# Softmax sums of six attention rows from pre-added quarters: GpSimd takes adds, VectorE's steps and the end of the program are dealt out anew

## The chip, the cores and the metric

The kernel runs on one core of a Trainium2 chip, as one program launched once. The metric is the device time of that launch in microseconds (us). The core's engines work from their own queues, each in program order, and wait for each other by semaphores: TensorE (PE in the profile; its weight loads are PEld), VectorE (DVE), ScalarE (ACT), GpSimd (POOL), SyncE (SP, which here only issues transfers). Transfers run on 16 DMA engines.

## The reference

Two transformer layers over eight sequences of 512 tokens, 128 wide, all in float32:

```python
x = L0_attn_x                                    # (8, 512, 128)
xn = _layernorm(x)
x = x + _L0_attn_ref(xn, ...) + _L0_ffn_ref(xn, ...)   # one head without softmax, then a norm; fp4-quantised ffn
xn = _layernorm(x)
x = x + _L1_attn_ref(xn, ...) + _L1_ffn_ref(xn, ...)
...
def _L1_attn_ref(x, Wq, bq, Wk, bk, Wv, bv, Wo, bo):    # 16 heads of 64, one shared key and value head
    q = (x @ Wq + bq).reshape(B, S, H, DK); k = x @ Wk + bk; v = x @ Wv + bv
    scores = jnp.einsum('bshd,btd->bhst', q, k) / np.sqrt(DK)
    w = jax.nn.softmax(scores, axis=-1)
    out = jnp.einsum('bhst,btd->bshd', w, v).reshape(B, S, H * DV)
    return out @ Wo + bo
def _L1_ffn_ref(...):                            # 8 experts, the top 2 of each token, hidden width 512
```

## The kernel before

The kernel is one long software pipeline. A **row** (index r, 0 to 7) is one sequence's layer-1 attention; it has 64 **steps** (index k): 16 heads by 4 quarters of 128 keys. Beside row r the layer-0 work of row r + 1 is strung out over the same steps, at places given by hand-written tables: `L0_AT` for TensorE and ScalarE, `L0_DVE` for VectorE (each entry k lets the generator `l0` run on to its next `yield` at step k). Row 7 also holds 92 steps of the expert feed-forward (23 tiles of tokens by 4, behind k = 15, 23 and 31). Every engine walks the same list `steps`, so the order of each queue is fixed when the program is built.

A step of attention is: `first` on TensorE (scores of a quarter, transposed, two matmuls, L1478 and L1479) into one of two PSUM banks; `Exp` on ScalarE into `wide`, a ring of six SBUF buffers 128x512 (L878). Two heads make a **pair**, eight steps, and their quarters alternate: even k is head b = 0, odd k is b = 1. Two steps behind each fourth step `values` takes four `wide` buffers at once: eight matmuls of weights with values (L1506, 32 columns of stationary data each, into four column groups) and then four matmuls with `ones`, 128x32, that add up the weights over the keys (L1517). A pair has two such blocks, so a row has 16. The last two pairs (`direct`) use eight ones matmuls a block (L1514) so that the sums come out spread over all partitions. In the profile each of these float32 matmuls shows as two records (x16 and x8 in a block).

When a pair is done, ScalarE copies the values bank (`raw`, L904) and one step later the sums bank (`sraw`, L909); SP sends the sums through DRAM, VectorE inverts them 16 wide (L1246, L1247), SP spreads them back (`inv`), and VectorE scales (`on`, L1260). For the direct pairs VectorE inverts the whole bank (L1264). `project` multiplies by Wo (L1538).

The row maximum for the exponent comes from a second set of scores (L1432) that VectorE reduces (`mneg`, L1066), two reductions at every other step, through a ring of four PSUM banks that also serves all of the layer-0 work; TensorE turns the maxima (L1437), ScalarE copies them and a transfer puts them beside the queries (`q_lm<-mrow`).

GpSimd computes inverse roots for the three norms of a row (`root`, L661: VectorE gives the variance at L952 and takes the root at L956), clears `x_rows` (L688), scatters routed tokens by indirect transfers (L702), and in row 0 subtracts the rounded half of 16 staged expert weights 128x512 (L726), whose inputs SP loads (`stage`) and whose results it stores (`w_rows`). At the start of row 7 SP loads the first four tiles' expert weights, 1 MB each (`WEIGHTS_AT`, `load_tile_weights`, L577), and GpSimd the first tiles' tokens `x_m`.

## Time and profile before

| | before |
|---|---|
| median of 3 runs | 1312.55 us (1308.25 to 1314.61) |
| profiled execution | 1308.08 us, span 1306.5 us |
| TensorE busy | 1220.1 us, 93% |
| VectorE busy | 955.3 us, 73% |
| ScalarE busy | 681.7 us, 52% |
| GpSimd busy | 264.3 us, 20% |
| TensorE clock, mean | 0.974 of full |

The span is the time from the first to the last instruction of the core; the profiled execution's own time is 1.58 us above it. Busy time counts an engine's instructions without its waits.

### The profile page before, as it was taken

The numbers are of one execution on the slowest core, as the hardware profiler recorded it, in microseconds if no ns is written. First come the engines' busy times: TensorE is split into PE (matmuls) and PEld (weight loads), VectorE is DVE, ScalarE is ACT, GpSimd is POOL, SyncE is SP. The second block draws the span as 40 slices with busy tenths as digits, with TensorE's granted clock in tenths as the row PEclk, the third lists the DMA queues.
The fourth block names the chain that finished last, engine by engine and source line by source line (L and its number), as shares of the span: only waits on it lengthen the run. The fifth ranks groups of instructions, "written<-read, shape, count | busy, mean of one in ns | idle before, by whom it ended". The sixth has DMA issues, their size and how long they took to land.

```text
span 1306.5 us, 21963 instructions
## 1 busy us (share of the span) xinstructions
PE 1220.1 (93%) x7185; PEld 722.9 (55%) x7185; DVE 955.3 (73%) x2332; ACT 681.7 (52%) x1252; POOL 264.3 (20%) x315
## 2 busy tenths in 40 slices
PE   5459989999999999999999999999999999999997
PEld 3235445555555555555554555555555458787743
DVE  6876787578857885788578857875687668677866
ACT  4136545644464456444644464456444468687731
POOL 2033222200220022002200220022000307273730
PEclk9669998999999999999999999999999989999999
DMA  3073666223422253225322432243222567476371
GB/s 81 1 194 97 205 195 194 75 72 78 139 67 67 68 147 75 67 67 139 83 67 67 140 83 67 66 140 83 67 67 67 146 202 241 153 248 198 120 218 59
DMA packets 99763, 150.59 MB, mean 115 GB/s; under 512 B 35340, under 2 KB 51276, under 8 KB 95684
## 3 DMA queue, kind: packets, MB, share of 16 engines
q1 hardware_dynamic: 84772, 115.53, 33.1%
q0 software_dynamic: 11664, 32.69, 7.8%
q10 hardware_dynamic: 3216, 0.97, 0.3%
q8 instruction: 59, 0.97, 0.3%
q14 instruction: 52, 0.43, 0.1%
HBM read 59.86 MB, written 38.68 MB: 75 GB/s over the span
## 4 chain that ended last, share of the span: by engine, by line
PE 66%; DVE 17%; DMA 4%; issue 4%; ACT 4%; POOL 2%; SPq 2%; ACTq 0%; DVEq 0%; POOLq 0%
PE bank L1506 14%; PE bank L1478 7%; PE bank L1517 6%; PE bank L1432 5%; PE bank L1479 5%; PE bank L1334 4%; PE bank L1336 4%; PE bank L1335 4%; DVE mneg L1066 4%; PE bank L1538 3%; PE bank L1350 2%; ACT wide L878 2%; PE bank L1340 2%; PE bank L1396 1%; PE bank L1375 1%
## 5 line engine op out<-in xcount | busy, mean ns | idle before, releaser
L878 ACT ACTIVATE wide<-bank 128x512 f32<-128x512 f32 x512 | 294.8, 599 | 319.5 <-PE bank L1479 319.2
L1066 DVE TENSOR_REDUCE mneg<-bank 128x1 f32<-128x512 f32 x512 | 328.8, 684 | 146.5 <-PE bank L1432 142.3
L1478 PE MATMUL bank<-q_hh,k_hl 128*128 128x512 f32 x512 | 233.5, 456 | 17.8 <-ACT wide L878 14.1
L1506 PE MATMUL bank<-wide,v_w 128*32 128x512 f32 x2048 | 248.1, 602 | 1.0 <-issue 1.0
L1479 PE MATMUL bank<-q_lm,k_h 65*128 65x512 f32 x512 | 203.8, 398 | 0.0
L1478 PEld LDWEIGHTS bank<-q_hh,k_hl 128*128 128x128 f32 x512 | 96.8, 189 | 139.8 <-issue 78.3
L661 POOL TENSOR_TENSOR rs<-rs,power 128x4 f32<-128x4 f32 x24 | 24.5, 1020 | 616.6 <-DVE rs L952 616.5
L1517 PE MATMUL bank<-wide,ones 128*32 128x512 f32 x992 | 129.1, 592 | 0.0
L740 POOL DMA_INDIRECT y_rows<-y_m,to_u x92 | 103.3, 1123 | 105.0 <-DVE y_m L1192 83.0
L1506 PEld LDWEIGHTS bank<-wide,v_w 128*32 128x32 f32 x2048 | 53.8, 109 | 123.0 <-issue 115.2
L1432 PE MATMUL bank<-k_a,q_x 128*128 128x512 f32 x256 | 106.5, 416 | 4.7 <-ACT hqt L798 2.7
L1432 PE MATMUL bank<-k_b,q_x 128*128 128x512 f32 x256 | 102.6, 401 | 4.2 <-DVE mneg L1066 4.2
L1479 PEld LDWEIGHTS bank<-q_lm,k_h 65*128 65x128 f32 x512 | 97.6, 191 | 11.3 <-issue 1.4
L702 POOL DMA_INDIRECT x_rows<-xr,slot_u x64 | 63.0, 984 | 164.1 <-DVE slot_u L1138 129.7
L904 ACT ACTIVATE raw<-bank 128x512 f32<-128x512 f32 x64 | 38.3, 598 | 100.2 <-PE bank L1517 91.0
L1300 DVE TENSOR_TENSOR part_l<-wide,part_h 128x512 fp32r<-128x512 f32 x92 | 61.9, 689 | 32.6 <-ACT wide L883 32.2
L883 ACT ACTIVATE part_h<-bank,b_t 128x512 fp32r<-128x512 f32 x92 | 63.4, 689 | 22.9 <-PE bank L1336 16.1
L1517 PEld LDWEIGHTS bank<-wide,ones 128*32 128x32 f32 x992 | 32.3, 110 | 74.6 <-issue 74.6
L1538 PE MATMUL bank<-wo,on 128*128 128x128 f32 x512 | 61.4, 279 | 4.8 <-DVE on L1260 4.8
L1538 PEld LDWEIGHTS bank<-wo,on 128*128 128x128 f32 x512 | 60.9, 195 | 7.4 <-DVE on L1260 6.2
L1432 PEld LDWEIGHTS bank<-k_a,q_x 128*128 128x128 f32 x256 | 49.0, 191 | 25.9 <-ACT q_x L808 12.8
L883 ACT ACTIVATE wide<-bank,b_t 128x512 f32<-128x512 f32 x92 | 63.0, 685 | 0.0
(253 smaller groups left out, 1938.4 us busy)
## 6 DMA issues: line engine op xcount, KB each, us to landing
q_hh<-q_x SPq DMA_DIRECT2D x256, 128.0 KB
w_t<-w_rows SPq DMA_DIRECT2D x23, 1024.0 KB, 4.7
x_rows<-part_h POOLq DMA_DIRECT2D x65, 258.0 KB, 5.0
q_lm<-q_rest SPq DMA_DIRECT2D x128, 128.0 KB
inv<-inverse_scratch SPq DMA_DIRECT2D x124, 128.0 KB, 2.9
w_rows<-w_t SPq DMA_DIRECT2D x8, 1024.0 KB, 5.0
x_m<-x_rows SPq DMA_DIRECT2D x19, 258.0 KB, 3.8
stage<-in_L_ffn_W SPq DMA_DIRECT2D x16, 256.0 KB, 4.9
```

Of the source, the lines that this page charges most:

```text
L702: pool.indirect_dma_start(x_rows, bass.IndirectOffsetOnAxis(ap=slot_u[:, b, i:i + 1], axis=0), xr[:, i, :], None).then_inc(scattered, 16)
L740: pool.indirect_dma_start(y_rows, bass.IndirectOffsetOnAxis(ap=to_u[:, t % TO, i:i + 1], axis=0), y_m[:, t % YM, i, :], None).then_inc(y_s ...
L878: act.activation(wide[:, st.g % WIDE, :], ps, ACT.Exp, scale=SCALE1).then_inc(wide_full, 1)
L883: ins = act.activation(dst, ps, ACT.Gelu_apprx_tanh, bias=b_t[:, st.t % WT, st.m:st.m + 1])
L1066: dve.tensor_reduce(mneg[:, pair % 2, col:col + 1], ps[:], X, ALU.max, negate=True).then_inc(free, 1)
L1300: dve.tensor_tensor(part_l[:, y % PARTS, :], wide[:, st.g % WIDE, :], part_h[:, y % PARTS, :].bitcast(F32), ALU.subtract).then_inc(lo_done, 1)
L1432: into(("mx", 2 * pair + b, j), lambda ps: pe.matmul(ps[:], q_x[:, pair % 2, P * j:P * j + P], keys[:, n % 2, :], start=True, stop=True))
L1478: pe.matmul(ps, k_hl[:, n, t], q_hh[:, gh % HEADS, :], start=True, stop=False)
L1479: last = pe.matmul(ps, k_h1[0:DK + 1, n, t], q_lm[0:DK + 1, gh % HEADS, :], start=False, stop=True)
L1506: pe.matmul(ps_out[0][rows, :], v_w[:, n, c, TILE * d:TILE * d + TILE], weights, start=(c == 0), stop=(c == TT - 1))
L1517: last = pe.matmul(ps_out[1][rows, :], ones[:], weights, start=(half == 0), stop=(half == 1))
L1538: last = pe.matmul(ps[:, P * i:P * i + P], on[:, g % (H // 4), P * i:P * i + P], wo[:, g, :], start=(g == pairs.start), stop=(g == pairs.s ...
```

## The change

In rows 1 to 6 (pairs 8 to 55, `added`) GpSimd adds, at each step with k % 4 of 2 or 3, the `wide` buffer of two steps earlier to the present one, as two instructions of 128x256 (`halve`), into `halves`. One step after the last values block of the pair TensorE does four ones matmuls on these sums (`sums_of`) in place of the eight that its two blocks had. ScalarE's `Exp` waits for the add before it overwrites a `wide` buffer, and its copy `sraw` moves one step back. GpSimd's program is dealt out over the steps: roots, scatters and clears stand at given steps among the adds. `halves` and `stage` lie over `x_m`, and the expert weights of row 0 turn over four buffers rather than two.

VectorE's table `L0_DVE` is new: the norm of layer-0 attention with its scale and shift runs at k = 5 to 8 rather than 29 to 37, the quantisation of `xn` starts at k = -4 rather than -7, and the variance of two norms is given out earlier. The turning of the maxima moves from the sixth to the fifth step of a pair. In row 7 the direct pairs do ones ahead of values, the last projection is split after pair 6 rather than 5, and three of the four first expert weights are loaded at k = -2, -1 and 1. Row 7 keeps its ones matmuls on `wide`.

```diff
-    LAST_NORM_AT = {6: ATT, 7: ATT + 3}
-    LAST_WO_AT = [None, ATT, ATT + 4]
+    LAST_NORM_AT = {6: ATT, 7: ATT + 2}
+    LAST_WO_AT = [None, ATT + 2, ATT + 3]
...
-    WEIGHTS_AT = [2, 5, 10, 12]
+    ROWS_AT, WEIGHTS_AT = 2, [-2, -1, 1, 13]
...
+    FIRST_HALVED, LAST_HALVED = H // 2, (NB - 1) * (H // 2)
+    ROOT_AT = [6, 42, 51]
+    SCATTER_AT = [[1, 4, 5, 8], [13, 16, 17, 20]]
+    ZERO_AT = [24, 25, 28, 29, 32, 33, 36, 37]
...
+    def added(pair):
+
+        return FIRST_HALVED <= pair < LAST_HALVED
...
+    def adds(st):
+
+        return st.kind == "o" and st.k % TT >= 2 and added(pair_of(st))
...
-        if s == TT + 1 and 0 <= here + 1 < total:
-            events.append(("mt", here + 1))
...
+        if s == TT and 0 <= here + 1 < total:
+            events.append(("mt", here + 1))
...
+            def halve(st):
+
+                half, b, pair = st.k % PAIR // TT, st.k % 2, pair_of(st)
+                if pair > FIRST_HALVED:
+                    pool.wait_ge(summed, pair - FIRST_HALVED)
+                pool.wait_ge(wide_full, st.g + 1)
+                for q in range(2):
+                    cols = slice(S // 2 * q, S // 2 * q + S // 2)
+                    last = pool.tensor_tensor(halves[:, half, b, cols], wide[:, (st.g - 2) % WIDE, cols],
+                                              wide[:, st.g % WIDE, cols], ALU.add)
+                last.then_inc(halved, 1)
...
                     if st.g >= WIDE:
                         act.wait_ge(second_done, st.g - WIDE + 1)
+                        if st.g - WIDE in add_of:
+                            act.wait_ge(halved, add_of[st.g - WIDE])
...
+            def sums_of(pair):
+
+                free_bank(("ps", pair))
+                pe.wait_ge(halved, add_of[last_step(2 * pair + 1)])
+                for half in range(2):
+                    for b in range(2):
+                        rows = slice(DK * b + TILE * half, DK * b + TILE * half + TILE)
+                        last = pe.matmul(ps_out[1][rows, :], ones[:], halves[:, half, b, :], start=True, stop=True)
+                last.then_inc(summed, 1)
...
-                pairs = (slice(0, 4), slice(4, 8 if r < NB - 1 else 6), slice(6, 8))[part]
+                pairs = (slice(0, 4), slice(4, 8 if r < NB - 1 else 7), slice(7, 8))[part]
...
+                pair = pair_end(st, 1)
+                if pair is not None and added(pair):
+                    sums_of(pair)
```

TensorE's queue at a pair's end in row 1, before: values (L1506) and ones (L1517) stand together after every fourth step.

```order
L1506 MATMUL bank<-wide,v_w 32x512 x8
L1517 MATMUL bank<-wide,ones 32x512 x4
L1478 MATMUL bank<-q_hh,k_hl 128x512
L1479 MATMUL bank<-q_lm,k_h 128x512
L1432 MATMUL bank<-k_a,q_x 128x512
L1432 MATMUL bank<-k_b,q_x 128x512
L1334 MATMUL bank<-x_h,wq_h 128x512
```

The same place in the changed kernel (L1589 is values, L1559 the ones matmuls of `sums_of`, L1536 and L1537 the scores):

```order
L1589 MATMUL bank<-wide,v_w 32x512 x8
L1536 MATMUL bank<-q_hh,k_hl 128x512
L1537 MATMUL bank<-q_lm,k_h 128x512
L1490 MATMUL bank<-k_a,q_x 128x512
L1490 MATMUL bank<-k_b,q_x 128x512
L1392 MATMUL bank<-x_h,wq_h 128x512
L1393 MATMUL bank<-x_l,wq_h 128x512
L1394 MATMUL bank<-x_h,wq_l 128x512
L1619 MATMUL bank<-wo,on 128x128 x16
L1559 MATMUL bank<-halves,ones 32x512 x4
```

The ones matmuls have left both blocks of the pair and stand once, a step behind the second.

VectorE's queue at the end of a row, before (L923 to L938 are the quantisation of `xn`, L1124 and L1126 the routing slots):

```order
L1118 TENSOR_TENSOR gsel<-gsel,gs 128x32
L923 TENSOR_REDUCE qs<-xn 128x32
L924 TENSOR_SCALAR qs<-qs 128x32
L925 RECIPROCAL qs<-qs 128x32
L927 TENSOR_SCALAR qs<-qs 128x32
L1124 TENSOR_TENSOR ahead<-ahead,bank 128x8 x4
L1126 TENSOR_TENSOR slot<-ahead,bank 128x32
L930 TENSOR_TENSOR t_66<-xn,qs 128x512
L932 TENSOR_SCALAR t_67<-t_66 128x512
L1066 TENSOR_REDUCE mneg<-bank 128x1 x2
L1059 SCALAR_TENSOR_TENSOR q_rest<-bank,bq_two,q_x 128x512
```

and in the changed kernel, where L1124 is now the reduction of maxima, L1182 and L1184 the slots, L982 to L991 the quantisation:

```order
L1176 TENSOR_TENSOR gsel<-gsel,gs 128x32
L1124 TENSOR_REDUCE mneg<-bank 128x1 x2
L1182 TENSOR_TENSOR ahead<-ahead,bank 128x8 x4
L1184 TENSOR_TENSOR slot<-ahead,bank 128x32
L1117 SCALAR_TENSOR_TENSOR q_rest<-bank,bq_two,q_x 128x512
L982 TENSOR_REDUCE qs<-xn 128x32
L983 TENSOR_SCALAR qs<-qs 128x32
L984 RECIPROCAL qs<-qs 128x32
L986 TENSOR_SCALAR qs<-qs 128x32
L989 TENSOR_TENSOR t_66<-xn,qs 128x512
L991 TENSOR_SCALAR t_67<-t_66 128x512
```

Six instructions of the quantisation have moved behind a pair of maxima and the rest of a query.

TensorE's queue at the very end, before (L1514 ones of a direct pair, L1538 projection):

```order
L1478 MATMUL bank<-q_hh,k_hl 128x512
L1479 MATMUL bank<-q_lm,k_h 128x512
L1538 MATMUL bank<-wo,on 128x128 x8
L1506 MATMUL bank<-wide,v_w 32x512 x8
L1514 MATMUL bank<-wide,ones 32x512 x8
L1538 MATMUL bank<-wo,on 128x128 x8
```

and now:

```order
L1536 MATMUL bank<-q_hh,k_hl 128x512
L1537 MATMUL bank<-q_lm,k_h 128x512
L1582 MATMUL bank<-wide,ones 32x512 x8
L1589 MATMUL bank<-wide,v_w 32x512 x8
L1619 MATMUL bank<-wo,on 128x128 x16
```

The ones come first, and all 16 matmuls of the second projection (12 for pairs 4 to 6, 4 for pair 7) stand behind the values.

## Rows read from the trace of the kernel before

**Rows 1.** Stretches: start:end, length, busy us of each engine, clock, DMA share

```profile
501.00:633.00 132.00, 130.01 (x803) 73.50 (x802) 97.76 (x249) 68.27 (x129) 15.61 (x22) 1.00 0.36 88
...
603.00:623.00 20.00, 19.91 (x134) 12.86 (x133) 17.08 (x57) 8.68 (x17) 5.57 (x10) 1.00 0.62 148
623.00:633.00 10.00, 10.00 (x53) 5.21 (x53) 7.30 (x22) 7.64 (x12) 3.28 (x4) 1.00 0.53 146
```

**Rows 2.** The chain that ended last, two rows' worth: start, us, what

```profile
490.83 1.98 PE bank L1350 x4
...
622.75 1.98 PE bank L1350 x4
```

**Rows 3.** The same chain from 600 to 732 us

```profile
600.43 0.86 PE bank L1517 x8
...
717.22 0.86 PE bank L1517 x8
...
718.98 0.30 DVE xres L1007
...
722.73 1.02 POOL rs L661
```

**Rows 4.** Groups of instructions: busy us, mean ns, idle before

```profile
L1517 PE MATMUL bank<-wide,ones 128*32 128x512 f32 x992 | 129.1, 592 | 0.0
...
L726 POOL TENSOR_TENSOR w_t<-stage,w_t 128x512 fp32r<-128x512 f32 x16 | 20.6, 1288 | 68.5 <-ACT w_t L847 68.5
```

**Rows 5.** Timeline of GpSimd in row 0: start, us, instruction

```profile
162.35 2.56 POOL L726 TENSOR_TENSOR w_t<-stage,w_t 128x512 fp32r<-128x512 f32 x2
```

**Rows 6.** Timeline of VectorE in the same stretch

```profile
127.22 1.49 DVE L937 TENSOR_TENSOR t<-t,t 128x352 f32<-128x352 f32 x1
128.74 0.52 DVE L938 TENSOR_TENSOR t<-t,t 128x352 f32<-128x352 f32 x1
...
162.39 1.23 DVE L956 SCALAR_TENSOR_TENSOR rs<-rs 128x4 f32<-128x4 f32 x1
163.66 1.27 DVE L957 TENSOR_TENSOR rs<-rs 128x4 f32<-128x4 f32 x1
164.96 0.16 DVE L958 SCALAR_TENSOR_TENSOR rs<-rs 128x4 f32<-128x4 f32 x1
...
188.40 1.20 DVE L952 TENSOR_SCALAR rs<-mv 128x4 f32<-128x4 f32 x1
```

**Rows 7.** Timeline of VectorE at the end of a row

```profile
618.39 0.69 DVE L923 TENSOR_REDUCE qs<-xn 128x32 f32<-128x512 f32 x1
...
621.54 0.43 DVE L932 TENSOR_SCALAR t<-t 128x512 uint32<-128x512 uint32 x1
```

**Rows 8.** Timelines of SP, VectorE and TensorE at the start of row 7

```profile
1035.38 0.38 SPq L577 DMA_DIRECT2D w_t<-w_rows  x1
...
1038.13 0.59 SPq L533 DMA_DIRECT2D sums_scratch<-sraw  x1
...
1046.74 0.17 DVE L1246 TENSOR_TENSOR sums<-sums 128x16 f32<-128x16 f32 x1 [8.28 <-DMA sums<-sums_scratch]
...
1047.80 0.79 PE L1432 MATMUL bank<-k_b,q_x 128*128 128x512 f32 x1 [4.15 <-DVE mneg L1066]
...
1050.57 3.24 PE L1506 MATMUL bank<-wide,v_w 128*32 128x512 f32 x16
```

**Rows 9.** Waits from 105 to 237 us: total us, times, longest

```profile
ACT w_t L847 <- DMA stage<-in_L_ffn_W: 18.0, 7, 6.6
```

**Rows 10.** Timeline of all engines at the end of the program

```profile
1289.73 2.05 PE L1538 MATMUL bank<-wo,on 128*128 128x128 f32 x16 [0.62 <-DVE on L1260]
1291.71 1.92 PE L1506 MATMUL bank<-wide,v_w 128*32 128x512 f32 x16
...
1293.45 1.90 PE L1514 MATMUL bank<-wide,ones 128*32 128x512 f32 x16
...
1295.44 3.36 DVE L1264 RECIPROCAL inv_d<-bank 128x512 f32<-128x512 f32 x1 [2.94 <-PE bank L1514]
...
1299.58 3.40 PE L1538 MATMUL bank<-wo,on 128*128 128x128 f32 x16 [4.23 <-DVE on L1260]
1303.03 0.69 DVE L1235 TENSOR_TENSOR xres<-xres,bank 128x512 f32<-128x512 f32 x1 [3.50 <-PE bank L1538]
```

More of the change, by code:

```diff
@@ L281, in two_layers @@
     ring = Ring(SMALL, small_order)
+    add_of, count = {}, 0
+    for st in steps:
+        if adds(st):
+            count += 1
+            add_of[st.g] = add_of[st.g - 2] = count
     out_place, out_uses = {}, [0] * OUTB
@@ L573, in load_tile_weights @@
                     sp.wait_ge(table_set, 1)
+                    for i in range(WT):
+                        sp.wait_ge(w_stored[i], E // WT * 16)
                 ew = sp.value_load(tb_u[0:1, 1, t:t + 1], min_val=0, max_val=E - 1)
@@ L708, in load_first_rows @@
                 pool.wait_ge(scattered, 2 * TT * NB * 16)
+                pool.wait_ge(summed, LAST_HALVED - FIRST_HALVED)
                 for t in range(XT):
@@ new lines, in _ @@
+            for n in range(2):
+                for e in range(E):
+                    zero(n, e)
+            root()
+            for st in steps:
+                if st.kind == "o":
+                    if st.k in (ROOT_AT if st.r < NB - 2 else ROOT_AT[0:2] if st.r == NB - 2 else ()):
+                        root()
+                    if adds(st):
+                        halve(st)
+                    if st.r == 0 and st.k in SPLIT_STEPS:
+                        split_rest(SPLIT_STEPS.index(st.k))
+                    for b, at_ in enumerate(SCATTER_AT if st.r < NB - 1 else LAST_SCATTER_AT):
+                        for i in range(TT):
+                            if st.k == at_[i]:
+                                scatter(st.r, b, i)
+                    if st.k in ZERO_AT and st.r + 2 < NB:
+                        zero(st.r + 2, ZERO_AT.index(st.k))
+                    if st.r == NB - 1 and st.k == ROWS_AT:
+                        load_first_rows()
+                if st.g is not None:
+                    here, i = divmod(st.g - 3, TT)
+                    if here - 2 in tile_of:
+                        scatter_y(tile_of[here - 2], i)
@@ L905, in _ @@
                 pair = pair_end(st, 1)
-                if pair is not None and not direct(pair):
+                if pair is not None and not direct(pair) and not added(pair):
                     act.wait_ge(second_done, last_step(2 * pair + 1) + 1)
+                    act.wait_ge(sums_stored[pair % 2], 16 * (pair // 2))
+                    act.activation(sraw[:, pair % 2, :], ps_out[1][:], ACT.Identity).then_inc(out_free[1], 1)
+                pair = pair_end(st, 2)
+                if pair is not None and added(pair):
+                    act.wait_ge(summed, pair + 1 - FIRST_HALVED)
                     act.wait_ge(sums_stored[pair % 2], 16 * (pair // 2))
@@ L1493, in values @@
                 if half == 0:
-                    for name in (("pv", pair), ("ps", pair)):
-                        b, uses = out_place[name]
-                        if uses:
-                            pe.wait_ge(out_free[b], uses)
+                    free_bank(("pv", pair))
+                    if not added(pair):
+                        free_bank(("ps", pair))
                     if st.k == TT - 1:
@@ L1500, in values, with weights @@
                 pe.wait_ge(wide_full, st.g + 1)
+                def weights(c, b):
+                    return wide[:, (st.g - 3 + 2 * (c % 2) + b) % WIDE, :]
+                if direct(pair):
+                    for c in range(2 * half, 2 * half + 2):
+                        for b in range(2):
+                            for d in range(2):
+                                rows = slice(DK * b + TILE * d, DK * b + TILE * d + TILE)
+                                last = pe.matmul(ps_out[1][rows, :], ones[:], weights(c, b), start=(c == 0), stop=(c == TT - 1))
+                    if half:
+                        last.then_inc(summed_up, 1)
@@ L1508, in values @@
+                        if added(pair) or direct(pair):
+                            last.then_inc(second_done, 1)
+                if added(pair) or direct(pair):
+                    return
                 for c in range(2 * half, 2 * half + 2):
                     for b in range(2):
-                        weights = wide[:, (st.g - 3 + 2 * (c % 2) + b) % WIDE, :]
-                        if direct(pair):
-                            for d in range(2):
-                                rows = slice(DK * b + TILE * d, DK * b + TILE * d + TILE)
-                                last = pe.matmul(ps_out[1][rows, :], ones[:], weights, start=(c == 0), stop=(c == TT - 1))
-                        else:
-                            rows = slice(DK * b + TILE * (c % 2), DK * b + TILE * (c % 2) + TILE)
-                            last = pe.matmul(ps_out[1][rows, :], ones[:], weights, start=(half == 0), stop=(half == 1))
@@ L1518, in values @@
-                        last.then_inc(second_done, 1)
+                        rows = slice(DK * b + TILE * (c % 2), DK * b + TILE * (c % 2) + TILE)
+                        pe.matmul(ps_out[1][rows, :], ones[:], weights(c, b), start=(half == 0), stop=(half == 1))\
+                            .then_inc(second_done, 1)
             def second(st):
@@ L1592, in _ @@
                     values(block_end(st))
+                pair = pair_end(st, 1)
+                if pair is not None and added(pair):
+                    sums_of(pair)
                 past = behind(st, LAG)
```

122 lines of the change are left out of this document (58 added, 64 removed).

## The prediction

> **What bounds the kernel now.** I read the busy times of whole rows first, then the chain that ended last, then the timelines of the places it passes. A row of attention repeats every 131.9 us (622.75 less 490.83, the same piece of the chain in two rows [rows 2]). In such a row TensorE is busy 130.0 of 132 us and VectorE 97.8 [rows 1]: TensorE bounds, with 2.0 us of idle time. The chain says the same for most of a row: 13 of its 16 blocks of ones matmuls lie on it, from 600.43 to 717.22, at 0.86 us each [rows 3]. But in two stretches it goes over VectorE: the end of the row, where VectorE is busy 17.1 of 20 us [rows 1], and some ten more from 718.98 on, with one hop over GpSimd's root of 1.02 us [rows 3]. TensorE is nearly full there too, so both engines are at the limit together. A faster TensorE meets VectorE in those 30 of 132 us first.
>
> **The change, part by part.**
>
> *Ones matmuls, rows 1 to 6.* A pair had two blocks of 0.86 us and gets one. That is 0.86 us of TensorE's work a pair, 6.9 a row, 41.3 in six rows. As a cross-check, all 124 such blocks take 129.1 us busy [rows 4], 1.04 each with the overlap at their ends. Only the 13 blocks on the chain count at once: 13 x 0.43 = 5.6 us a row. The other three lie under VectorE.
>
> *GpSimd's adds.* Each row has 32 adding steps of two instructions of 128x256. The nearest row is its subtraction 128x512 at 1.288 us [rows 4]; half of that is 0.64 us, so 64 x 0.64 = 41 us a row. The upper bound is that a short one costs what the root on 128x4 costs, 1.02 us [rows 3], 65 us a row. I take 0.64: the subtraction shows a cost that goes with its columns, and the root is another operation. With its present 15.6 us [rows 1] GpSimd is busy 57 to 81 of some 126 us. An Exp overwrites the buffer four steps after the add may start, 4 x 2.06 = 8.2 us, against 1.3 to 2.0 for a step's two adds and 1 or 2 us of a scatter or a root in front of them. I charge 0.5 us a row for late adds.
>
> *What the adds do to VectorE.* The trace shows two engines in each other's way. While two subtractions run on GpSimd from 162.35 for 2.56 us [rows 5], two VectorE instructions on 128x4, with inputs from SBUF, take 1.23 and 1.27 us where their successor takes 0.16, and at 127.22 one takes 1.49 where its twin takes 0.52 [rows 6]. The wait shows inside the duration. From 127.22 to 188.40 I find 8 such instructions, 6.2 us too long in total, beside 15 subtractions: 0.41 us for each. An add of half the length is met half as often and for half as long (0.10 us), or just as often for half as long (0.21 us): 6.6 to 13.1 us a row in 64 adds. VectorE's load rises from 97.8 to between 104 and 111 us. In the 30 of 132 us on the path that is 1.5 to 3.0 us; I take 2.1. The Trainium skill, "SBUF — State Buffer", section "Who interferes with whom", says that a VectorE instruction with two SBUF inputs, or in a two-port mode, and a GpSimd instruction that reads SBUF shut each other out for a whole instruction, whichever starts first; the stretched rows agree. By its letter the wait is at most one add, 0.64 us, which is the end of my range and not beyond it. The same skill, "GPSIMD Engine Reference", section 4.1, advises against elementwise work on GpSimd as about twice as slow; here its slowness matters only if the queue is late.
>
> *VectorE dealt out anew.* The six instructions of the quantisation that leave the end of the row take 3.58 us from first to last with the slots between them [rows 7], of which 2.5 are theirs. The variance of two norms goes out earlier, so two hops over GpSimd of about 1.1 us (one is the 1.02 us [rows 3]) fall away. That would be 4.7 us of VectorE's stretches. TensorE lies close underneath: its 2.0 us idle and the three hidden blocks' 1.3 us are all that can be won, 3.3. With 2.1 us of waits for GpSimd against 4.7, the net is -2.6. The 2.5 us go to the next ten microseconds, where VectorE is busy 7.3 [rows 1]; with 0.7 us of new waits it has 10.5 us of work in 9.1, so 1.3 us come back. Net -1.3 a row. The norm of attention moves from k = 29 to 37, where the chain is TensorE's, to k = 5 to 8, where it is too: nothing by itself, room for the new waits. In the remaining 100 us of a row some 7.5 us of new waits lie in VectorE's idle time; if that cover were gone they would cost all of it. I charge 1.0.
>
> Sum of a row: -5.6 - 1.3 + 0.5 + 1.0 = -5.4 us, six rows **-32.4 us**. The later `sraw` leaves five steps, ten microseconds, to the sums' way through DRAM: nothing. The turning of maxima one step earlier waits for a reduction that the ring of banks asks for at the same step anyway: nothing.
>
> *End of the program.* Before, projection (2.05), values (1.92), ones (1.90), then VectorE's inversion of 3.36 us while TensorE stands idle 4.23 us and comes back slow, 3.40 us for a projection whose twin took 2.05, then an addition of 0.69 [rows 10]. Now the block starts at about 1289.8 without the projection in front: ones to 1291.6, inversion to 1295.0, scaling to 1295.7; meanwhile values to 1293.5 and twelve matmuls of projection (2.7 us, by the 16 records' 1.8 for eight) to 1296.2, then four (0.9) to 1297.1, addition to 1297.8. The old addition ends at 1303.7: **-5.9 us**. The first direct pair's inversion can start 0.6 us earlier, before VectorE's own work holds it: **-0.6**.
>
> *Start of row 7.* SP issues a 1 MB weight load at 1035.38, directly in front of the sums' store at 1038.13; VectorE gets them at 1046.74 after 8.28 us of waiting, TensorE stands 4.15 us and then runs a values block in 3.24 us instead of 1.92 [rows 8]. The loss is 4.15 + 1.3 and about 1.3 more on neighbours, some 6.8 us. The three loads now start at k = -2, some 12 us ahead of the store. GpSimd's loads of `x_m` stay. I take **-5.0**, between 0 (the three loads queue up in front of it all the same) and -6.8.
>
> *Row 0.* 2 MB of clears move into the steps where expert weights are staged, for which ScalarE waits 18.0 us already [rows 9]. Bounds 0 and 5 us; **+1.5**, as the four buffers may take a wait away.
>
> Total: -32.4 - 5.9 - 0.6 - 5.0 + 1.5 = -42.4 us. The span of 1306.5 becomes 1264.1, the execution's 1308.08 becomes 1265.7. The median of the runs before is 4.5 us above its profiled execution, the fastest run equal to it; I keep **1266 us**.
>
> **The rivals.**
>
> *All of TensorE's saving is real* (0.14). VectorE's idle time takes every wait: -6.9 x 6 - 6.5 - 6.8 = -54.6, 1253 us. For it speaks that VectorE idles 34 of 132 us; against it that in 603 to 623 it idles only 3 [rows 1].
>
> *VectorE becomes the bound in longer stretches* (0.22). Half of the upper 13.1 us, 6.6, lies on the path instead of 3.1: +3.5 a row, +21, 1287 us. For it speaks the load of 111 in 126 us, 88%, and a ring of four banks that lets TensorE run ahead by only one pair of maxima.
>
> *VectorE bound throughout: slower* (0.07). Place: VectorE against the adds; price: all 13.1 us a row on the path, and some 4 us of its own maxima held up behind them, 17.1 instead of 3.1: +84 - 42, 1350 us. It decides when the waits on the path pass 3.1 + 42.4/6 = 10.2 us a row. Against it speaks that the maxima's reductions (one PSUM input) are nowhere stretched in row 0.
>
> *GpSimd's queue holds the Exp* (0.05): a root or scatter waits in order for VectorE, and adds behind it. It costs what exceeds the 8.2 us; at 3 us for each of three roots a row, 54 us, 1320 us, slower by 0.6%. Less of it, 1 us each, gives 1284.
>
> **How the numbers follow.** The forecast (0.52) has its own range 1258 to 1277. The range for all is 1252 to 1290: it takes in the first two rivals and leaves out under 2 in 10. Within 0.5% (6.6 us), about what a measurement of this kernel can tell from no change, lie only parts of the last two: 0.03. Slower: the third rival and some of the last, 0.09. Faster: 0.88.
>
> **What would show it.** Right: a row period near 126.5 us, 192 fewer ones matmuls, adds of about 0.64 us, TensorE idle 3 to 4 us a row, single VectorE instructions of 0.16 us stretched to 0.5 to 0.8, the last inversion ending 3.8 us earlier with TensorE busy beside it, no idle time of 4 us near the start of row 7. Wrong: Exp waiting for `halves`; reductions of maxima as long chains in the middle of rows; adds of 1 us; a period above 129.

## The result, and the profile after

The changed kernel takes 1317.86 us (median of 6 runs, 1316.16 to 1320.66), the kernel before, run beside it, 1312.42 us (6 runs, 1308.25 to 1314.61). The ratio is 1.005, 95% interval 1.0036 to 1.0063: half a per cent slower, where 1266 us was forecast. The profiled execution has a span of 1314.3 us, 7.8 more than before.

The page: busy us, share of the span, instructions; then the chain's shares and the group of the adds (busy us, mean ns | idle before).

```profile
PE 1207.7 (92%) x6801; PEld 704.0 (54%) x6801; DVE 1012.3 (77%) x2332; ACT 683.2 (52%) x1252; POOL 551.0 (42%) x699
...
PE 70%; DVE 19%; issue 4%; DMA 3%; ACT 2%; POOL 2%; SPq 1%; ACTq 0%; DVEq 0%; POOLq 0%
...
L744 POOL TENSOR_TENSOR halves<-wide 128x256 f32<-128x256 f32 x384 | 290.2, 780 | 369.7 <-PE bank L1559 217.8
```

TensorE lost 12 us of work, VectorE has 57 us more with no instruction of its own added, GpSimd 287 more. The stretches that answer to [rows 1], and two in the middle of the next row:

```profile
501.00:633.00 132.00, 126.76 (x744) 70.83 (x742) 108.63 (x252) 70.08 (x133) 64.63 (x86) 1.00 0.33 89
603.00:623.00 20.00, 19.37 (x125) 12.52 (x124) 17.32 (x50) 10.25 (x20) 8.57 (x12) 1.00 0.24 55
623.00:633.00 10.00, 10.00 (x54) 4.86 (x51) 9.41 (x26) 6.42 (x11) 4.08 (x6) 1.00 0.18 58
662.00:670.00 8.00, 6.95 (x39) 2.97 (x32) 7.69 (x18) 3.53 (x7) 3.31 (x5) 1.00 0.08 24
670.00:680.00 10.00, 7.24 (x39) 3.23 (x41) 9.83 (x16) 3.39 (x8) 8.34 (x10) 0.95 0.50 136
```

VectorE goes from 97.8 to 108.6 us in 132. The end of the row is now no tighter than the middle: from 662 to 680 VectorE has half a microsecond free, TensorE stands, and the mean granted clock of the last stretch is 0.95. Taken by itself, the piece behind the stall runs at half the clock, which is the lower of its two levels, 1.2 GHz:

```profile
678.90:682.30 3.40, 3.40 (x18) 0.60 (x16) 3.19 (x9) 1.03 (x3) 0.96 (x1) 0.50 0.14 44
```

In the chain, the same piece of projection in two following rows:

```profile
499.29 2.64 PE bank L1408 x6
...
629.68 2.65 PE bank L1408 x6
...
761.68 2.67 PE bank L1408 x6
```

It returns after 130.4 and 132.0 us, against 131.9 in [rows 2]; the chain's row jitters by a place, so below I use score matmuls: their first step in rows 1 and 6 starts at 248.1 and 907.0, against 239.3 and 899.0 before. A row takes **131.8 us; it took 131.9**. Six rows gave nothing.

Where the 7.8 us arose, from the start of the first score matmul of steps (after less before, us; the parts are rounded). Here and below such a stretch is read from one profiled execution of each kernel, which lies up to 4.5 us from the median of its runs:

| stretch | forecast | measured |
|---|---|---|
| row 0 | +1.5 | +8.8 |
| rows 1 to 6 | -32.4 | +0.3 |
| row 7, k = 0 to 16 | -5.0 | +3.2 |
| row 7, k = 16 to 56 | 0 | +2.1 |
| from there to the end | -6.5 | -6.5 |

Inside a row the gain is there and is lost again: from k = 24 to 48 a row wins 3.4 us, from k = 56 to 64 0.9, and from k = 16 to 24 it loses 4.2. The timeline of all engines there (start, us, instruction, idle before); it answers to nothing in [rows 3], since before this place was TensorE's alone:

```profile
659.71 2.80 POOL L744 TENSOR_TENSOR halves<-wide 128x256 f32<-128x256 f32 x4 [2.56 <-ACT wide L932]
659.77 0.69 DVE L1015 SCALAR_TENSOR_TENSOR rs<-rs 128x4 f32<-128x4 f32 x1
660.50 0.66 DVE L1016 TENSOR_TENSOR rs<-rs 128x4 f32<-128x4 f32 x1
661.18 0.66 DVE L1017 SCALAR_TENSOR_TENSOR rs<-rs 128x4 f32<-128x4 f32 x1
...
673.71 3.79 POOL L744 TENSOR_TENSOR halves<-wide 128x256 f32<-128x256 f32 x4 [0.83 <-ACT wide L932]
673.74 1.09 DVE L997 TENSOR_TENSOR t<-t,t 128x352 f32<-128x352 f32 x1
674.86 0.93 DVE L1000 TENSOR_TENSOR sg<-t,qs 128x352 f32<-128x352 f32 x1
675.72 1.21 DVE L1318 TENSOR_TENSOR on<-raw,inv 128x512 f32<-128x512 f32 x1
676.85 1.27 DVE L1124 TENSOR_REDUCE mneg<-bank 128x1 f32<-128x512 f32 x2
677.58 0.86 PE L1460 MATMUL bank<-wu,xqt 128*128 128x352 f32 x2 [2.76 <-DVE mneg L1124]
...
679.34 3.39 PE L1589 MATMUL bank<-wide,v_w 128*32 128x512 f32 x16
```

While four adds run (0.70 us each), each 128x4 instruction of VectorE lasts almost as long as an add, where it took 0.16 us before; the larger ones behind them are stretched too. The maxima of the next pair (L1124) come behind them; TensorE stands 2.76 us for these, and its next block of values takes 3.39 us instead of 1.92.

### The profile page after: what moved, and what is told of

It is laid out like the page before. It is cut to its first block, busy times and chain, and to the rows that moved or that the text cites. A ratio compares the mean times of both kernels' runs of the same rounds, so it can differ in the third digit from the quotient of the medians.

```text
span 1314.3 us, 21803 instructions
## 1 busy us (share of the span) xinstructions
PE 1207.7 (92%) x6801; PEld 704.0 (54%) x6801; DVE 1012.3 (77%) x2332; ACT 683.2 (52%) x1252; POOL 551.0 (42%) x699
## 4 chain that ended last, share of the span: by engine, by line
PE 70%; DVE 19%; issue 4%; DMA 3%; ACT 2%; POOL 2%; SPq 1%; ACTq 0%; DVEq 0%; POOLq 0%
PE bank L1589 15%; PE bank L1536 8%; PE bank L1537 6%; PE bank L1490 6%; DVE mneg L1124 5%; PE bank L1392 5%; PE bank L1619 4%; PE bank L1394 4%; PE bank L1393 4%; PE bank L1559 3%; PE bank L1408 2%; PE bank L1398 2%; PE bank L1443 2%; PE bank L1454 2%; PE bank L1433 1%
## 5 line engine op out<-in xcount | busy, mean ns | idle before, releaser
L932 ACT ACTIVATE wide<-bank 128x512 f32<-128x512 f32 x512 | 298.2, 598 | 337.7 <-PE bank L1537 305.1
L744 POOL TENSOR_TENSOR halves<-wide 128x256 f32<-128x256 f32 x384 | 290.2, 780 | 369.7 <-PE bank L1559 217.8
L1124 DVE TENSOR_REDUCE mneg<-bank 128x1 f32<-128x512 f32 x512 | 328.3, 682 | 128.8 <-PE bank L1490 125.0
L1589 PE MATMUL bank<-wide,v_w 128*32 128x512 f32 x2048 | 257.4, 622 | 0.0
L1536 PE MATMUL bank<-q_hh,k_hl 128*128 128x512 f32 x512 | 239.3, 467 | 15.4 <-ACT wide L932 12.6
L1537 PE MATMUL bank<-q_lm,k_h 65*128 65x512 f32 x512 | 205.2, 401 | 0.0
L1536 PEld LDWEIGHTS bank<-q_hh,k_hl 128*128 128x128 f32 x512 | 97.3, 190 | 155.0 <-issue 82.4
L752 POOL DMA_INDIRECT y_rows<-y_m,to_u x92 | 98.0, 1066 | 103.1 <-DVE y_m L1250 81.7
L1589 PEld LDWEIGHTS bank<-wide,v_w 128*32 128x32 f32 x2048 | 55.5, 112 | 132.0 <-issue 124.9
L1537 PEld LDWEIGHTS bank<-q_lm,k_h 65*128 65x128 f32 x512 | 98.5, 192 | 9.4 <-issue 1.4
L860 ACT ACTIVATE q_x<-bank,bq_two 128x512 fp32r<-128x512 f32 x64 | 44.0, 687 | 45.9 <-PE bank L1394 45.4
L1490 PEld LDWEIGHTS bank<-k_b,q_x 128*128 128x128 f32 x256 | 49.1, 192 | 24.0 <-DVE mneg L1124 12.8
```

The lines of the kernel that those rows point to most:

```text
L744: last = pool.tensor_tensor(halves[:, half, b, cols], wide[:, (st.g - 2) % WIDE, cols], wide[:, st.g % WIDE, cols], ALU.add)
L752: pool.indirect_dma_start(y_rows, bass.IndirectOffsetOnAxis(ap=to_u[:, t % TO, i:i + 1], axis=0), y_m[:, t % YM, i, :], None).then_inc(y_s ...
L932: act.activation(wide[:, st.g % WIDE, :], ps, ACT.Exp, scale=SCALE1).then_inc(wide_full, 1)
L1124: dve.tensor_reduce(mneg[:, pair % 2, col:col + 1], ps[:], X, ALU.max, negate=True).then_inc(free, 1)
L1490: into(("mx", 2 * pair + b, j), lambda ps: pe.matmul(ps[:], q_x[:, pair % 2, P * j:P * j + P], keys[:, n % 2, :], start=True, stop=True))
L1536: pe.matmul(ps, k_hl[:, n, t], q_hh[:, gh % HEADS, :], start=True, stop=False)
```

## The experiments

**Adds almost taken away; the deal taken back; the deal alone.** The first leaves GpSimd's adds and waits in place and cuts each to 4 columns, so most of the sums are left out; in the first added pair it fills the rest of `halves` with ones:

```diff
+                if pair == FIRST_HALVED:
+                    for q in range(2):
+                        pool.memset(halves[:, half, b, S // 2 * q + 4:S // 2 * q + S // 2], 1.0)
...
-                    cols = slice(S // 2 * q, S // 2 * q + S // 2)
+                    cols = slice(S // 2 * q, S // 2 * q + 4)
```

> The changed kernel with each of GpSimd's adds cut from 256 columns to 4, all waits and semaphores kept (the sums of weights of rows 1 to 6 are then wrong: nearly all of halves keeps the value 1). It takes away the time that the adds hold VectorE and leaves the new deal of VectorE's work. Theory A, the waits for GpSimd's adds eat the saving: VectorE busy falls from 108 to about 98 us a row, the stalls of TensorE at steps 10 to 12 and 16 to 18 vanish, the row's period falls from 132.0 to about 126, the whole to about 1283 us. Theory B, the new deal packs too much of VectorE's work into steps 5 to 17 and would stall without any add: the period stays at 130 or above, the whole above 1305 us.

The second has VectorE's work at its old steps, in the changed kernel; the third has it at the new steps, in the kernel before, with one root in row 0 moved ahead to match:

```diff
-    L0_DVE = [-14, -13, -11, -10, -4, -4, -3, -2, 0, 0, 5, 6, 7, 8, 8, 10, 11, 13, ...
-    ROOT_AT = [6, 42, 51]
+    L0_DVE = [-14, -11, -11, -10, -7, -6, -4, -2, 0, 0, 9, 10, 13, 17, 18, 21, 25, ...
+    ROOT_AT = [30, 43, 53]
...
-                if n:
-                    yield from attended(18)
-                    yield 18
-                    scale_and_shift()
...
```

> The changed kernel with the old table of VectorE's steps, the norm of attention back at steps 29 to 37 and GpSimd's roots at steps 30, 43 and 53 to match; the adds stay whole. Theory A: waits for the adds stay and fall elsewhere, period 130 to 132, the whole about 1315 us. Theory B: steps 5 to 17 have room again, no stall at step 16, period about 127 to 128, the whole about 1290 us.

> The kernel before with the new deal of VectorE's work alone (GpSimd's second root in row 0 moved to before its first subtraction, so that nothing waits in a circle). Theory A: without adds the deal does no harm, period 131 to 132, the whole 1308 to 1313 us. Theory B: the stall at step 16 is there without adds, period 134 to 136, the whole 1325 us or more.

Measured: 1285.93 us without most of the adding (ratio to the kernel before 0.979, 0.977 to 0.981); 1357.71 with the old deal (1.033, 1.031 to 1.035); 1312.24 for the new deal alone (1.000, 0.998 to 1.001). The adds therefore cost 32 us. Rows 1 to 6 take 758.8 us without real adds, 784.0 before and 784.3 in the changed kernel: 25.5 of the 32 us lie there, all that these rows had saved, and 5.6 more in steps 0 to 16 of row 7 (81.4 us against 87.1). The deal is worth nothing by itself and 40 us beside the adds: theory B, that it causes a stall without any add, fell. The result with the old deal was in neither theory's range. The deal does decide where the adds' waits stop TensorE: with the old one steps 16 to 24 take 16.2 us (16.8 before the change), but steps 32 to 40 take 18.8 (15.9) and steps 56 to 64 27.1 (20.9; means of rows 1 to 5). With the old deal a row takes 140.0 us ((935.38 - 375.47) / 4 in the chain, the same piece of projection), and that piece itself runs slow:

```profile
375.47 5.23 PE bank L1409 x6
...
935.38 5.17 PE bank L1409 x6
```

**The size of an add.** The three kernels differ from the changed one only in the pieces of a step's add; the sums are the same.

```diff
-                for q in range(2):
-                    cols = slice(S // 2 * q, S // 2 * q + S // 2)
+                for q in range(4):
+                    cols = slice(S // 4 * q, S // 4 * q + S // 4)
```

> The changed kernel with each add as four instructions of 128x128 rather than two of 128x256. The total of columns is the same. If VectorE waits for the rest of one GpSimd instruction: the single wait halves (at most some 0.43 instead of 0.73 us), but GpSimd's fixed cost of 0.15 us a piece makes it busy 9 to 10 us a row more; VectorE busy a row falls from 107 to about 104 us, the whole 5 to 15 us faster. If VectorE waits for the whole stream of adds (GpSimd takes the pair back at once): VectorE's busy time stays or rises and the whole is 1318 us or slower.

> The changed kernel with each add as one instruction of 128x512. If VectorE waits for the rest of one GpSimd instruction: single waits of up to 1.28 us, VectorE busy a row rises from 107 to 109 to 112 us, the whole 5 to 20 us slower. If it waits for the whole stream: no change within 4 us.

> The changed kernel, each step's adds in eight instructions of 128x64 instead of two of 128x256. The same sums. So far 512 columns gave 1335, 256 gave 1318, 128 gave 1293 us, and adds of 4 columns (two a step) 1286. Theory (VectorE's small instructions wait for the rest of one GpSimd instruction, so its length sets the price): an add should take about 0.30 us (0.45 for 128 and 0.73 for 256 columns give 0.16 us fixed and 0.0022 a column), eight 2.4 us a step, GpSimd busy about 95 us a row, and each wait is at most 0.3 us: 1283 to 1293 us. Rival 1 (what counts is the share of time in which GpSimd works, since each new instruction can slip in ahead of VectorE): more waits, not shorter ones in sum, 1293 to 1320. Rival 2: GpSimd's queue gets late, as 2.4 us a step with a root or a scatter is more than a step of 2.06 us: over 1300, and ScalarE or the ones matmuls wait for the sums.

One row of each in its trace, from 633 us on, with the adds of 512, 256, 128, 64 and 4 columns in this order (start:end, length, busy us of TensorE, weight load, VectorE, ScalarE, GpSimd, clock, DMA):

```profile
633.00:767.16 134.16, 126.08 (x729) 69.81 (x733) 108.95 (x247) 68.27 (x129) 58.43 (x53) 0.99 0.32 87
```

```profile
633.00:764.79 131.79, 126.58 (x738) 70.07 (x737) 107.05 (x249) 68.28 (x130) 64.14 (x85) 0.99 0.33 89
```

```profile
633.00:761.41 128.41, 125.13 (x738) 69.89 (x738) 104.78 (x249) 68.52 (x130) 74.81 (x150) 1.00 0.34 91
```

```profile
633.00:762.04 129.04, 125.14 (x738) 69.62 (x737) 108.05 (x249) 68.44 (x129) 96.82 (x278) 1.00 0.35 90
```

```profile
633.00:761.15 128.15, 124.63 (x738) 70.37 (x737) 97.57 (x248) 68.86 (x130) 28.96 (x86) 1.00 0.34 91
```

| columns of an add | time, us | ratio to before | row, us | VectorE's waits a row |
|---|---|---|---|---|
| 512 | 1335.36 | 1.019 (1.016 to 1.022) | 134.2 | 11.4 |
| 256 | 1317.86 | 1.005 (1.004 to 1.006) | 131.8 | 9.5 |
| 128 | 1292.90 | 0.985 (0.984 to 0.987) | 128.4 | 7.2 |
| 64 | 1295.32 | 0.987 (0.984 to 0.991) | 129.0 | 10.5 |
| 4 (sums left out) | 1285.93 | 0.979 (0.977 to 0.981) | 128.2 | 0 |

The last column is VectorE's busy time less the 97.57 us of the row without real adds. One reads two things. The waits are 7 to 11 us whatever the length; what they cost the row is 6.0, 3.6, 0.3 and 0.9 us. And TensorE's own busy time in the same 738 matmuls is 124.63 without adds and 126.58 with those of 256: of the 3.6 us, 2.0 are matmuls that run longer, and the 3.4 us at half the clock account for 1.7 of them. The quarters gained 25 us, more than the 5 to 15 expected; whole adds lost 17, as expected. Below 128 columns nothing more is won, and the two times do not differ clear of their intervals: an add of 64 still takes 0.316 us (0.453 for 128), GpSimd works 97 of 129 us, and VectorE's waits rise from 7.2 to 10.5 us. So the theory of the length was right in direction, and its 1283 to 1293 for 64 columns was a little too low; the measured time lies in the range of rival 1, the share of time. The 7 us between 128 and 4 columns lie mostly at the start of row 7, whose steps 0 to 16 take 88.4, 87.1, 86.1, 85.9 and 81.4 us in the order of the table. There an add's length matters little.

**Row 0's clears.** They go from steps 24 to 37, among the staging of expert weights, to 54 to 61:

```diff
+                    zero_at = ZERO_AT if st.r else [54, 55, 56, 57, 58, 59, 60, 61]
```

> The changed kernel with GpSimd's eight clears of row 0 moved from steps 24 to 37 to steps 54 to 61, behind the staging of expert weights. If the clears delay the staged weights (ScalarE waited 7.12 us for one at 160.9): the 7.2 us that row 0 loses between steps 32 and 34 vanish and the whole is about 1311 us. If the staging waits for something else (the stores of 1 MB, the turning over four buffers): no change, 1318 us.

1315.51 us (1.002, 0.9998 to 1.003). Row 1 begins 2.9 us late instead of 8.8, so the clears are 6 of the 8.8 in this pair of traces. In all traces, row 1 begins at 247.0 to 250.6 us in the nine kernels with the new adds and the early clears, and at 242.0 to 244.9 in the five with late ones. By the medians the whole kernel got 2.4 us of it, less than the 7 of the first theory. In the changed kernel's row 0 ScalarE waits for a staged weight, an Exp stands behind it in its queue, and TensorE waits for that:

```profile
168.00 0.63 ACT L899 ACTIVATE w_t<-stage 128x512 fp32r<-128x512 f32 x1 [7.12 <-DMA stage<-in_L_ffn_W]
...
169.16 0.80 PE L1536 MATMUL bank<-q_hh,k_hl 128*128 128x512 f32 x1 [7.03 <-ACT wide L932]
```

**The maxima turned one step later, as before.**

```diff
-        if s == TT and 0 <= here + 1 < total:
+        if s == TT + 1 and 0 <= here + 1 < total:
```

> The changed kernel with the turning of maxima back at the sixth step of a pair. At the end of row 7 TensorE waits 3.05 us for a reduction before it (step 52), as VectorE still adds expert outputs. If that wait is new with the earlier place: the 2.9 us between steps 52 and 53 of row 7 vanish, rows 1 to 6 move by under 0.5 us each, the whole about 1315 us. If VectorE is the bound wherever the turning stands: the 2.9 us stay and the whole is 1318 us.

1322.29 us (1.007, 1.005 to 1.010). The wait that it was to remove is this one, in row 7 of the changed kernel, and it went:

```profile
1279.55 0.29 PE L1495 MATMUL bank<-ident,mneg 128*8 128x128 f32 x1 [3.05 <-DVE mneg L1124]
1280.63 3.12 PE L1582 MATMUL bank<-wide,ones 128*32 128x512 f32 x16
```

But another came in its place, five steps earlier, for the transfer of the turned maxima, with slow matmuls behind it:

```profile
1278.99 0.77 PE L1536 MATMUL bank<-q_hh,k_hl 128*128 128x512 f32 x1 [2.26 <-DMA q_lm<-mrow]
```

Steps 44 to 56 of row 7 take 26.0 us with the late turning and 26.2 with the early one, and the whole of row 7 281.9 and 282.0: in the last row the place of the turning is worth nothing. Rows 1 to 5 got 1.7 us longer each (133.5), row 6 1.5 shorter. Neither number of the expectation (1315, 1318) came out, and the ratio's interval overlaps that of the changed kernel.

**The start of row 7 as before.**

```diff
-    TABLE_CUTS = [59, 59, 60, 61]
-    ROWS_AT, WEIGHTS_AT = 2, [-2, -1, 1, 13]
+    TABLE_CUTS = [58, 59, 59, 62]
+    ROWS_AT, WEIGHTS_AT = 2, [2, 5, 10, 12]
```

> The changed kernel with the tiles' table computed at steps 58, 59, 59 and 62 and the first expert weights loaded at steps 2, 5, 10 and 12 of row 7, as before. If the table's chain on VectorE and the three early loads of 1 MB cost the start of row 7: the 9.7 us that it loses up to step 10 shrink to the 5 us that the kernel before lost at step 12, the whole 3 to 6 us faster, about 1313 us. If the late start is only VectorE's general delay by the adds: no change, 1318 us.

1317.77 us (1.003, 1.001 to 1.005): as the changed kernel. Steps 0 to 16 of row 7 took 86.4 us, against 87.1 changed and 83.9 before. Without real adds they took 81.4: it is the adds again that ate a gain of 2.5 us, by which way is open.

**No adds where the stall is.** Pairs 1 and 2 of rows 1 to 6 keep their 16 ones matmuls:

```diff
-        return FIRST_HALVED <= pair < LAST_HALVED
+        return FIRST_HALVED <= pair < LAST_HALVED and pair % (H // 2) not in (1, 2)
```

> The changed kernel without adds for the second and third pair of each row 1 to 6 (steps k = 8 to 23), whose sums go over 16 ones matmuls in TensorE again, as before the change; the adds of the other six pairs as they are (128x256). The same sums. TensorE gets 2 x 0.86 = 1.7 us a row of work back. Theory (the price is paid at one place, where VectorE is busy without a gap from k = 16 to 24 with the norm of attention and the quantisation, and TensorE loses 4 to 5 us there and part of its clock): the stall goes, a row costs 132 + 1.7 - 4.5 = 129, 6 rows 17 us less, 1300 us. Rival (VectorE is behind over the whole row, and the stall moves to the next tight place): the row keeps 132 or gets 1.7 us longer, 1318 to 1328 us.

1304.23 us (0.992, 0.989 to 0.996), a row 130.0 us. Steps 16 to 24 take 16.8 us again, as before the change (21.0 changed); steps 8 to 16 take 15.9, where both kernels took 13.5 to 14.0. So about half of the stall moved to the steps ahead, and neither theory's number came out (1300, or 1318 and more). Its five runs spread from 1297.9 to 1308.6 us, and the profiled one is the slowest. The place was rightly named, though: the row won 1.8 us with a quarter of the adds gone, and that beside giving up a quarter of the saving of 3.8, or 1.7 us if one counts the two blocks at 0.86. By this estimate these adds carried 2.8 to 3.5 us of a price of 3.6.

**The improvements together.**

> The changed kernel with three edits that seemed good one by one: adds in four instructions of 128x128 (1293 alone), the eight clears of row 0 at steps 54 to 61 (row 1 then began 6 us earlier, end 2 us earlier), and the turning of the maxima one step later, in the last row alone, as before the change (the wait of 3 us before the transposition vanished when it was done for all rows, but each row lost 1.3). The output is the reference's. If the three are independent: 1293 - 5 - 2.5 = 1285 us. If row 1 waits for VectorE whatever precedes it, the clears give only 2 us and the sum is 1289. If none adds up, 1293. Slower than before (over 1313) would say that the clears disturb the shorter adds.

1290.52 us (0.984, 0.980 to 0.987), 2.4 less than the quarters alone: the edits do not add up to the 7 us hoped for. In the traces row 1 begins 3.5 us earlier than with the quarters alone, which is the clears; row 7 takes 281.0 us against 281.2, so the late turning there gave next to nothing. In the profile of this kernel the start of row 7 still takes 86.6 us, and the last four scatters and the loads of tile rows are late. Three more kernels build on it. The first leaves the last pair of row 6 out of the adding, the second issues the tiles' weights later, the third does both:

```diff
-    FIRST_HALVED, LAST_HALVED = H // 2, (NB - 1) * (H // 2)
+    FIRST_HALVED, LAST_HALVED = H // 2, (NB - 1) * (H // 2) - 1
...
-    ROWS_AT, WEIGHTS_AT = 2, [-2, -1, 1, 13]
+    ROWS_AT, WEIGHTS_AT = 2, [2, 5, 10, 12]
```

> The kernel with quarters of 128x128, row 0's clears at steps 54 to 61 and the late turning in the last row (1290.5 us), and in it the last pair of row 6 without adds: its sums go over 16 ones matmuls again. The output is the reference's. In the profiles, the last four scatters of tokens stand in GpSimd's queue behind that pair's last adds (first scatter 2.7 us after the slots are there, against 1.0 before the change) and the rows of the first tile are loaded 25.6 us after row 7 began, against 14.6 before. Theory Q (GpSimd's order is what makes row 7 begin its tiles late): 0.9 us more of ones matmuls, scatters 2 to 3 us earlier, net 1 to 2 us less: 1288.5 to 1289.5. Rival D (the landing of scatters among 3 MB of weights sets it, or the first tile is not on the path at all): 1290.5 to 1291.5.

> The kernel with quarters of 128x128, row 0's clears at steps 54 to 61 and the late turning in the last row (1290.5 us), and in it the weight loads of the first three tiles issued at steps 2, 5 and 10 of row 7, as before the change, instead of -2, -1 and 1. The output is the reference's. In the profile of the changed kernel SP waits for the table of tiles with the loads (1040.49 to 1047.67) while the next pair's queries are ready at 1044.1; their DMAs are issued at 1047.78, and TensorE waits 2.5 us for them. Theory S (the waits of SP for the table hold the queries behind them): that wait of TensorE vanishes, the begin of the second pair of row 7 comes 2 to 3 us earlier; if the sums' way does not become late in its place, 1287.5 to 1288.5. Rival (the loads come later and meet the sums' store and load again, as in the kernel before, where VectorE waited 8.28 us for them): 1290.5 or up to 3 us more.

> The two edits before it together, over the same three: the last pair of row 6 without adds, and the weight loads at steps 2, 5 and 10 of row 7. The output is the reference's. If both theories hold: 1290.5 - 1.5 - 2.5 = 1286.5 us. If neither, 1291. If the second alone, 1289.

The kernel before took 1316.84 us beside these (1311.9 to 1319.01). One edit: 1293.83 us (0.983, 0.981 to 0.986); the other: 1295.30 (0.985, 0.982 to 0.987); both: **1289.81 us (0.980, 0.978 to 0.982)**, the best of the kernels that compute all sums. The expectations had 1287.5 to 1293.5 for the single edits and 1286.5 to 1291 for both. Alone, neither moved the ratio from the 0.984 they built on; steps 0 to 16 of row 7 took 88.2 and 87.8 us. Both together: 82.5. GpSimd and SP in that kernel:

```profile
1011.02 0.98 POOL L729 DMA_INDIRECT x_rows<-xr,slot_u  x1 [0.28 <-POOL xr L723]
...
1012.11 2.41 SPq L588 DMA_DIRECT2D q_hh<-q_x  x4
...
1016.82 0.37 SPq L610 DMA_DIRECT2D w_t<-w_rows  x1
...
1019.25 0.60 POOL L764 DMA_DIRECT2D x_m<-x_rows  x1 [3.46 <-issue]
```

and in the changed kernel, where row 7 begins 27.2 us later:

```profile
1040.49 0.38 SPq L608 DMA_DIRECT2D w_t<-w_rows  x1
...
1047.66 0.98 POOL L727 DMA_INDIRECT x_rows<-xr,slot_u  x1 [0.28 <-POOL xr L721]
...
1047.78 2.56 SPq L586 DMA_DIRECT2D q_hh<-q_x  x4
...
1058.19 0.59 POOL L762 DMA_DIRECT2D x_m<-x_rows  x1 [5.76 <-issue]
```

Counted from the row's first score matmul (1005.2 and 1032.4), the queries' DMA goes out at 6.9 instead of 15.4 us and the tile's rows are loaded at 14.0 instead of 25.8, ahead of most of the weights. What row 7 gained there, 4.1 us, it gave back behind k = 16 (174.5 us to k = 56, against 170.0 in the kernel without the two edits). Why is open. In the trace the kernel with both edits is 1.0 us shorter only because its row 1 begins 2.3 us earlier, and neither edit stands in row 0. So the gain of the last 0.4% is not shown to be theirs; the intervals of the ratios overlap too.

## Why the prediction was wrong, step by step

**The gross saving of a row: 5.6 us of ones matmuls and 3.3 of the end of the row.** This is the step that failed first, with 4.4 us a row, or 26 us of the 50 between forecast and result. Without waits for adds my sum would have been about -8 us a row; the kernel whose adds cost VectorE nothing (97.6 us busy, as before) is 3.8 shorter. TensorE did shed 5.3 us a row (129.9 to 124.6), near my 5.6, but its idle time rose from 2.0 to 3.5. Most of that is waits for the transfer that puts the turned maxima beside the queries, which the row before the change did not have (what waits for what: us in total, times, longest):

```profile
PE bank L1539 <- DMA q_lm<-mrow: 2.6, 3, 1.0
```

The gain of the end of the row, which I put at 3.3 before the waits, was not there: steps 56 to 64 became 0.9 us shorter, as much as their one block of ones, and the deal alone moved nothing. I had read a chain through VectorE as time that VectorE's work, moved away, gives back, and had set against it the 2.0 us that TensorE idles in a whole row. Of these only 0.09 us lie in the 20 us of the row's end and none in the 10 behind them [rows 1], and 0.5 in VectorE's other stretch, in the row before the change:

```profile
585.00:603.00 18.00, 17.52 (x110) 9.33 (x102) 13.26 (x40) 10.54 (x19) 1.01 (x1) 1.00 0.35 90
```

So there was little for the deal to give back. The matmuls themselves went as announced: the 384 instructions that TensorE's line of the page has lost are 192 matmuls, two records each.

**GpSimd's adds: 0.64 us each, 0.5 us a row for late ones.** They take 0.73 us (713 to 1193 ns), as some 0.18 us of each does not go with its columns (by the medians for 256 and 512 columns). Nobody waits for them, but ScalarE for 2.4 us in the whole program:

```profile
ACT wide L932 <- POOL halves L744: 2.4, 3, 0.8
```

The 0.5 was too much, and the rival of GpSimd's queue fell.

**The adds' waits on VectorE: 6.6 to 13.1 us a row, of which 2.1 in its stretches and 1.0 in the rest of the row lie on the path.** The size was right: 9.5 us. The price is 3.6 instead of 3.1, and it lies elsewhere. I had called the norm of attention at k = 5 to 8 "where the chain is TensorE's", "room for the new waits". It is there that VectorE, full from 659 to 680 with the norm, the first quantisations and the waits, got late: I had taken the room from a kernel in which this work did not yet lie there. Steps 16 to 24 lost 4.2 us, the end of the row nothing. And in the row shown 2.0 of the 3.6 us are TensorE's slower matmuls behind the stall, a term that [rows 8] and [rows 10] had shown me and that I charged only there. Over rows 1 to 6 TensorE is busy 753.3 us, against 741.8 without real adds: 11.5 of the 25.5 us. The rival of VectorE in longer stretches had the mechanism, at a price of 6.6 that was too high; the two misses together made no change out of a gain of 32 us.

**Row 0: +1.5, bounds 0 and 5.** Measured +8.8, of which some 6 are the clears. The row that I read, ScalarE waiting 18.0 us for staging DMAs [rows 9], grew to 24.8, by about the size of the loss; with the clears moved it is 19.2:

```profile
ACT w_t L899 <- DMA stage<-in_L_ffn_W: 24.8, 7, 7.1
```

I had bounded the cost by the clears' own bytes and not by the wait that was already there, with TensorE behind it.

**Start of row 7: -5.0.** Measured +3.2. Without real adds it is -2.5. The weight loads do leave ahead of the sums' store, but SP waits for the table with them, and the next queries stand behind them: the very question "what is queued behind a waiting instruction", which I had put for ScalarE and GpSimd and not for SP. GpSimd's scatters stand behind the last adds, and its second four wait 6.20 us for the first four to land (1.46 in the kernel with both edits). Taking the last adds away and issuing the weights later were each tried alone, on top of the quarters, and gave steps 0 to 16 nothing back (88.2 and 87.8 us); both together gave 82.5. So the two together are shown to delay the start of the row, and what each does is not.

**The maxima turned a step earlier: nothing.** Beside the adds it gains 1.7 us in each of rows 1 to 5, loses 1.5 in row 6 and is worth nothing in row 7, where the wait only changed its place.

**End of the program: -5.9 and -0.6.** Right: -6.5 from k = 56 on. The last inversion runs beside values and projection, as worked out:

```profile
1303.47 1.92 PE L1582 MATMUL bank<-wide,ones 128*32 128x512 f32 x16 [0.70 <-ACT wide L932]
...
1305.21 1.90 PE L1589 MATMUL bank<-wide,v_w 128*32 128x512 f32 x16
1305.46 3.36 DVE L1322 RECIPROCAL inv_d<-bank 128x512 f32<-128x512 f32 x1 [1.53 <-PE bank L1582]
...
1307.04 3.84 PE L1619 MATMUL bank<-wo,on 128*128 128x128 f32 x32
...
1310.91 0.69 DVE L1293 TENSOR_TENSOR xres<-xres,bank 128x512 f32<-128x512 f32 x1 [0.21 <-PE bank L1619]
```

The projection runs without a stop behind it, where TensorE stood 4.23 us and came back slow in [rows 10].

## What to carry to other kernels

Work moved to an idle engine can be paid for by another one that it shuts out, here VectorE: before moving it, count the small instructions of that engine in the tight stretches **as they will lie after the change**, and price each at one whole instruction of the new work. Then cut the new instructions so short that such a wait is bearable (here 128 columns: 25 us for a change of two lines), but not so short that their fixed part fills the engine (64 columns gave no more). When a saving on the bounding engine comes out small, look for the stall that took its place and for the slow matmuls behind it, which here were nearly half of the price in rows 1 to 6.

## What the runs showed of the hardware

VectorE and GpSimd take turns by whole instructions. The same addition on 128x4, nine times in three rows (min/median/max ns, first and last start), with adds of 4, 64, 128, 256 and 512 columns on GpSimd:

```profile
L1019 DVE TENSOR_TENSOR rs<-rs x9: 161/161/165, 523.9 to 864.0; 128x4 f32<-128x4 f32 x9
```

```profile
L1016 DVE TENSOR_TENSOR rs<-rs x9: 242/245/246, 523.1 to 866.6; 128x4 f32<-128x4 f32 x9
```

```profile
L1016 DVE TENSOR_TENSOR rs<-rs x9: 380/381/384, 522.7 to 864.7; 128x4 f32<-128x4 f32 x9
```

```profile
L1016 DVE TENSOR_TENSOR rs<-rs x9: 161/607/657, 530.1 to 882.0; 128x4 f32<-128x4 f32 x9
```

```profile
L1016 DVE TENSOR_TENSOR rs<-rs x9: 161/1202/1206, 533.5 to 892.8; 128x4 f32<-128x4 f32 x9
```

The adds' own medians are 198, 316, 453, 729 and 1281 ns. From 64 columns up the small instruction, where it is stretched, lasts as long as one add less 0.07 to 0.08 us (245, 381, 657 and 1206 ns). Of three such in a row each takes that long: after each add one VectorE instruction gets in, and the next waits for nearly a whole add, where my expectations had it wait for whatever is left of one. The Trainium skill, "SBUF — State Buffer", section "Who interferes with whom", says that a VectorE instruction with two SBUF inputs and a GpSimd instruction that reads SBUF contend, and that whoever starts first keeps the ports that they share for the whole instruction. The trace agrees; that the two take turns is seen in the trace alone. Reductions of maxima with their input in PSUM are not touched: 681 ns in the median with adds of 4 columns, 681 with 128 and with 512. The same skill's "GPSIMD Engine Reference", section 4.1, advises against elementwise work on GpSimd for its slowness; here only ScalarE waited for the adds themselves, 2.4 us in all, and the 25.5 us of rows 1 to 6 came with VectorE's waits.
